# First FFN chunk's inputs and 28 weight tiles loaded in attention's last chunk, and the head of the FFN stage taken row tile by row tile

## The chip, the cores and the metric

One Trainium2 chip, one core. The metric is the device time of one execution in microseconds (us). Rows and times of the profile come from one profiled execution, and `L1301` means line 1301 of the kernel before. The engines are PE (TensorE; its weight loads are listed as PEld), DVE (VectorE), ACT (ScalarE), POOL (GpSimd) and SP (SyncE, which here only issues DMAs; its issues are listed as SPq). TensorE's granted clock is 1.00 at 2.4 GHz and 0.50 at 1.2 GHz.

## The reference

A transformer layer on x of 4096 rows by 512 columns, in float32:

```
q, k, v = split(x @ Wqkv);  q, k = layernorm(q) * q_scale, layernorm(k) * k_scale    # over all 512 columns
ctx = softmax(causal(q_h @ k_h.T / sqrt(32))) @ v_h      for each of 16 heads of 32 columns
x   = layernorm(x + ctx @ out_W)
h   = silu(x @ Wg.T) * (x @ Wu.T)       # Wg, Wu: 2048x512 integers minus 128, times a scale per row
x   = layernorm(x + h @ Wd.T)           # Wd: 512x2048, made in the same way
```

## The kernel before

The kernel is three stages, each a block of five instruction streams, with a barrier of all engines between them. `project` makes q, k and v and writes them to DRAM, each in a high and a low part, and turns the 48 integer weight tiles of the FFN (16 inner tiles by gate, up and down, 256 KB each) into floats in DRAM (`wq`). `attend` runs four groups of four heads; in each it takes the 8 query chunks of 512 rows in order, and for chunk n the key blocks of 128 rows up to the diagonal, so that the last chunk has 32 steps. A step is two score products, two exponentials on ACT, the weighting with the values on PE, and a sum on DVE (`total`). Key blocks of 512 rows lie in SBUF (`keys`, 64 KB per partition) with three query buffers (`queries`, 8 KB each); SP reloads each for the next group once its last scores are made. `store` sends a chunk's context and its sums to DRAM; the sums of chunk 0 are inverted inside `attend`, those of chunks 1 to 7 in `finish`.

`finish` is the FFN stage, in 8 chunks of 512 rows. A chunk has 16 inner tiles ("ic": gate and up into two `slot` banks at L1301, Silu on ACT at L1372, the product with up and the split on DVE at L1457 to L1465, and the down product into the four `y` banks at L1312). The first half of the layer for the next chunk is placed between the inner tiles ("o": output projection L1275, "t": transposes L1285). For chunk 0 nothing lies ahead to place it in, so it stands as a head in front. Its steps are these:

- SP loads the context (`cp_lo`, L1156), the inverses spread over partitions (`y_raw`, L1167), the residual rows (`x_res`, L1161), the scales, and then the weights, tile by tile (L1196, L1201).
- DVE scales the context (`context`: L1406, cast L1408, low part L1410) in two halves of 256 rows; each half raises `c_ready`.
- PE projects a half: 24 products of 128x512 into two banks (12 for each 128 rows).
- DVE adds the residual (L1437), takes the statistics (L1416 to L1421), POOL the root (L1243), DVE normalises (L1426).
- PE transposes a half, ACT writes the high part (L1353), DVE the low part (L1449), which frees the `slot` banks for the first gate product.

Ahead of its first inner tile PE loads a flag (`value_load`, L1339) and branches to one of two copies of the whole FFN program, with or without full float32 products; the flag is made at the start of `finish` from the weights' largest magnitude (L1391 to L1397). ACT waits for the inverses of chunks 1 to 7 (`inv_stored`) before its first Silu, since they pass through the tile `hidden`.

## Time and profile before

| | us |
|---|---|
| median of 3 runs | 2382.1 (2381.18 to 2382.73) |
| the profiled execution | 2378.85 |
| its span, first to last instruction | 2377.1 |
| last product of attention ends | 1531.06 |
| first projection product of the head | 1546.34 |
| first gate product | 1572.41 |
| first down product | 1581.79 |

PE is busy for 2304.8 us of the span (97%), DVE 75%, ACT 54%, POOL 10%. `project` takes some 330 us, `attend` some 1200, `finish` some 845. From 1581.79 on the chain that ends last is PE alone apart from short pieces: an inner tile of gate, up and down takes 5.44 us each time. All times in the text count from the start of the span.

### The profile page before, as it was taken

How to read it: one execution, taken by the hardware profiler on the slowest of the kernel's cores; microseconds unless marked ns; L12 is line 12 of the kernel's file. 1: busy time of each engine (PE TensorE's matmuls, PEld its weight loads, DVE VectorE, ACT ScalarE, POOL GpSimd, SP SyncE). 2: the span in 40 equal slices, each digit the busy share in tenths (PEclk: the TensorE clock that was granted, in tenths of full speed). 3: DMA queues.
4: the chain of work that ended last, by engine and by line, in shares of the span. 5: the costliest groups of instructions: out<-in, count | busy, mean ns of one | idle time of the engine just before them, and what ended most of it. 6: DMA issues, size and time to landing. Idle time of an engine off the chain costs nothing. (4 is left out here: it accounts for less than half of the span.)

```text
span 2377.1 us, 34417 instructions
## 1 busy us (share of the span) xinstructions
PE 2304.8 (97%) x12578; PEld 1421.6 (60%) x12578; DVE 1775.6 (75%) x1822; ACT 1291.7 (54%) x1631; POOL 246.1 (10%) x269
## 2 busy tenths in 40 slices
PE   8999979999999999999999999789999999999997
PEld 7888844444444444444444444268888888888885
DVE  7767748998889988899888998745646556565554
ACT  4444458888888888888888888611111111111111
POOL 2111111110111101211011110000000000000000
PEclk9999989999999999999999999989999999999998
DMA  7767794101811008110081100181111021110100
GB/s 253 255 238 251 236 259 97 44 6 24 169 46 44 8 22 171 42 45 11 19 174 42 42 14 6 52 285 36 36 36 54 19 72 36 37 53 18 36 18 18
DMA packets 126879, 197.52 MB, mean 83 GB/s; under 512 B 15064, under 2 KB 40152, under 8 KB 126688
## 3 DMA queue, kind: packets, MB, share of 16 engines
q1 hardware_dynamic: 126704, 195.25, 28.9%
q8 instruction: 102, 1.67, 0.3%
q14 instruction: 73, 0.60, 0.1%
HBM read 122.83 MB, written 72.37 MB: 82 GB/s over the span
## 5 line engine op out<-in xcount | busy, mean ns | idle before, releaser
L968 ACT ACTIVATE probs<-score 128x1024 f32<-128x1024 f32 (+3 forms) x1152 | 1000.1, 969 | 174.3 <-PE score L880 172.3
L1031 DVE TENSOR_TENSOR total<-total,probs 128x2048 f32<-128x2048 f32 (+3 forms) x468 | 983.6, 2102 | 79.5 <-POOL probs L842 22.1
L880 PE MATMUL score<-queries,keys 98*128 98x512 f32 (+3 forms) x2304 | 641.4, 406 | 11.6 <-issue 6.5
L880 PEld LDWEIGHTS score<-queries,keys 98*128 98x128 f32 x2304 | 380.3, 189 | 433.4 <-ACT probs L968 350.0
L1372 ACT ACTIVATE hidden<-slot,gate_scale_sb 128x512 f32<-128x512 f32 x128 | 88.3, 690 | 624.7 <-PE slot L1301 624.7
L896 PE MATMUL ctx_acc<-probs,values 128*32 128x512 f32 (+3 forms) x3584 | 421.5, 561 | 0.0
L1457 DVE SCALAR_TENSOR_TENSOR hidden<-slot,up_scale_sb,hidden 128x512 f32<-128x512 f32 x128 | 96.0, 750 | 258.4 <-ACT hidden L1372 258.4
L842 POOL TENSOR_SCALAR_AFFINE_SELECT probs<-probs 128x512 f32<-128x512 f32 x128 | 167.5, 1310 | 1005.7 <-ACT probs L968 1005.7
L1301 PE MATMUL slot<-xt_hi,wg_sb 128*128 128x512 f32 x512 | 201.6, 394 | 5.2 <-issue 5.2
L896 PEld LDWEIGHTS ctx_acc<-probs,values 128*32 128x32 f32 x3584 | 85.4, 108 | 193.9 <-issue 148.9
L1312 PE MATMUL y<-wd_sb,h_hi 128*128 128x512 f32 x512 | 199.4, 389 | 1.4 <-DVE h_lo L1465 1.4
L1301 PE MATMUL slot<-xt_lo,wg_sb 128*128 128x512 f32 x512 | 200.0, 391 | 0.0
L1312 PE MATMUL y<-wd_sb,h_lo 128*128 128x512 f32 x512 | 199.3, 389 | 0.0
L1301 PE MATMUL slot<-xt_hi,wu_sb 128*128 128x512 f32 x512 | 199.2, 389 | 0.0
L1301 PE MATMUL slot<-xt_lo,wu_sb 128*128 128x512 f32 x512 | 199.2, 389 | 0.0
L344 PE MATMUL acc<-w_hi,x_hi 128*128 128x512 f32 x384 | 163.4, 425 | 7.2 <-DVE w_lo L495 7.2
L344 PE MATMUL acc<-w_hi,x_lo 128*128 128x512 f32 x384 | 150.9, 393 | 0.0
L344 PE MATMUL acc<-w_lo,x_hi 128*128 128x512 f32 x384 | 150.4, 392 | 0.0
L896 PE MATMUL ctx_acc<-probs,first_values 128*32 128x512 f32 (+3 forms) x1024 | 132.2, 588 | 0.7 <-ACT ctx_out L957 0.7
L1243 POOL TENSOR_TENSOR rstd<-veps,minus_half 128x1 f32<-128x1 f32 x64 | 36.7, 573 | 803.2 <-DVE veps L1421 803.2
L1301 PEld LDWEIGHTS slot<-xt_hi,wg_sb 128*128 128x128 f32 x512 | 96.7, 189 | 25.6 <-issue 5.6
L1312 PEld LDWEIGHTS y<-wd_sb,h_hi 128*128 128x128 f32 x512 | 96.1, 188 | 22.1 <-DVE h_lo L1465 2.2
(103 smaller groups left out, 2066.8 us busy)
## 6 DMA issues: line engine op xcount, KB each, us to landing
keys<-k_hi SPq DMA_DIRECT2D x64, 256.0 KB
queries<-q_hi SPq DMA_DIRECT2D x64, 256.0 KB
wq_int<-in_wq SPq DMA_DIRECT2D x48, 256.0 KB, 3.2
wq_float<-wq_f SPq DMA_DIRECT2D x48, 256.0 KB, 2.8
x_raw<-in_x_t SPq DMA_DIRECT2D x32, 256.0 KB, 3.6
v_rows<-v_out SPq DMA_DIRECT2D x32, 256.0 KB, 2.2
q_hi<-part_hi SPq DMA_DIRECT2D x32, 256.0 KB, 2.5
q_lo<-part_lo SPq DMA_DIRECT2D x32, 256.0 KB, 2.8
```

The costliest lines, as they stand in the source:

```text
L344: ins = pe.matmul(bank[:], x[:, par, dc, rows], w[:, dc, m * D:(m + 1) * D], start=dc == 0 and a == 0, stop=dc == DC - 1 and a == 2)
L842: pool.affine_select(out=view, in_=view, compare_op=ALU.is_ge, fill=0.0, base=0, pattern=[[0, HG], [1, P]], channel_multiplier=-1).then_in ...
L880: ins = pe.matmul(score[u % RING][:, i, cut(t):], keys[0:ROWS, kb // ST, h, kb % ST * P:(kb % ST + 1) * P], queries[0:ROWS, q_buffer[ch], ...
L896: ins = pe.matmul(ctx[h * HD:(h + 1) * HD, n0:], value(kb)[:, h * HD:(h + 1) * HD], probs[:, t % PB, h, n0:], start=t in first, stop=t in ...
L968: act.activation(probs[:, t % PB, 2 * p:2 * p + 2, cut(t):], score[u % RING][:, :, cut(t):], ACT.Exp).then_inc(exped, 1)
L1031: dve.tensor_tensor(into, into, now, ALU.add).then_inc(added, 1)
L1243: pool.tensor_tensor(rstd[:, k, st:st + 1], veps[:, k, st:st + 1], minus_half[:], ALU.pow).then_inc(rooted[k], 1)
L1301: ins = pe.matmul(slot[pos % 2][q][:], v(w[:, i, dc * P:(dc + 1) * P]), v(x[:, par, dc, :]), start=dc == 0 and a == 0, stop=dc == DC - 1 a ...
L1312: ins = pe.matmul(y[st][:], v(x[:, i % 2, st * P:(st + 1) * P]), v(wd[:, i, :]), start=i == 0 and a == 0, stop=i == IC - 1 and a == 1)
L1372: act.activation(hidden[:, i % 2, :], slot[pos % 2][0][:], ACT.Silu, scale=gate_scale[:, i:i + 1]).then_inc(gated, 1)
L1457: dve.scalar_tensor_tensor(hid, slot[pos % 2][1][:], up_scale[:, i:i + 1], hid, ALU.mult, ALU.mult)\
```

## The change

- The context, residual rows and inverses of chunk 0, and the first 7 blocks of four weight tiles each (28 of 48 tiles), are issued by SP inside `attend`'s last group. They go to the places of what has just been used for the last time: query buffers 0 and 1, and `keys`, one 8 KB block for each weight block. The other 5 weight blocks are loaded in `finish`, as 1 MB DMAs.
- The scales are loaded after group 0 of attention.
- The store of attention's last chunk moves behind the barrier, to the start of `finish`.
- Both flags are made at the end of `project`: one more reduction on DVE, a second transpose, and a reduction of twice the length.
- In the head PE loads its flag and branches at once, ahead of the head. The head goes by row tiles of 128 into the `y` banks, each with a semaphore of its own, and not by halves.
- The sums of chunks 1 to 7 pass through the second `x1` buffer, so that ACT has no wait on their inverses; DVE inverts them after the head, and waits for the store in the residual of chunk 1.

```
+def ctx_load(sp, dr, keep, n, h):
+    sp.dma_start(keep["cp_lo"][:, h, :, :].bitcast(F32),
+                 dr["ctx"].rearrange("(g r) s -> r g s", r=P)[:, :, bass.ds(n * CH + h * HC, HC)]).then_inc(keep["ctx_in"][h], 16)
...
+def inv_load(sp, dr, keep, n):
+    for h in range(HG):
+        sp.dma_start(keep["y_raw"][h * HD:(h + 1) * HD, :, :],
+                     dr["inverse"].rearrange("n (g h) s -> n h g s", h=HG)[bass.ds(n, 1), h, :, :]
+                     .to_broadcast([HD, NG, CH])).then_inc(keep["inv_ready"], 16)
...
+def weight_load(sp, dr, keep, to, j):
+    sp.dma_start(to.bitcast(F32), dr["wq"].rearrange("(b t) p d -> b p t d", t=ST)[j]).then_inc(keep["w_in"][j], 16)
...
+            dve.wait_ge(whole_done, 2 + WT * NCH)
+            dve.tensor_reduce(check[:, 1:2], whole[:], AX.X, ALU.max).then_inc(fin, 1)
...
+            dve.tensor_reduce(check_top[:], turn[0][0:1, 0:2 * P].rearrange("a (k p) -> a k p", k=2), AX.X, ALU.max).then_inc(fin, 1)
...
+                if g == NG - 1:
+                    sp.wait_ge(scored, 2 * NS * g + 2 * (last[NCH - 2] + 1) + Q_CREDIT)
+                    sp.nop(nofuse=True)
+                    for h in range(HALF):
+                        ctx_load(sp, dr, keep, 0, h)
+                    for h in range(HALF):
+                        x_load(sp, io, keep, 0, h)
+                store_chunk(sp, dr, keep, g, NCH - 2)
...
+            sp.dma_start(keep["gate_scale"][:], io["gate_scale"]).then_inc(keep["small_in"], 16)
+            sp.dma_start(keep["up_scale"][:], io["up_scale"]).then_inc(keep["small_in"], 16)
+            sp.dma_start(keep["whole"][:], io["down_scale"].rearrange("(a h) -> a h", a=1).to_broadcast([P, D]))\
+              .then_inc(keep["small_in"], 16)
...
-            store(sp, NG - 1, NCH - 1)
             sp.wait_ge(inverse_stored, 16 * NG + 16)
+            sp.nop(nofuse=True)
+            sp.wait_ge(scored, 2 * NS * (NG - 1) + 2 * (key_end[NCH - 1] + 1) + Q_CREDIT)
+            sp.nop(nofuse=True)
+            inv_load(sp, dr, keep, 0)
+            for b in range(2):
+                sp.wait_ge(keep["wq_stored"][b], 16 * (3 * IC // 2) + 16)
+            for j in range(FRONT):
+                sp.wait_ge(scored, 2 * NS * (NG - 1) + 2 * (key_end[j] + 1) + Q_CREDIT)
+                sp.nop(nofuse=True)
+                weight_load(sp, dr, keep, keep["w_front"][:, j * ST:(j + 1) * ST, :], j)
...
-            ctx_load(sp, 0, 0)
-            inv_load(sp, 0)
-            ctx_load(sp, 0, 1)
-            x_load(sp, 0, 0)
-            x_load(sp, 0, 1)
+            store_chunk(sp, dr, keep, NG - 1, NCH - 1)
             for b in range(2):
                 sp.wait_ge(keep["ctx_stored"][b], 32 * (NCH // 2) * NG + 32)
             sp.dma_start(sums_flat[:, REST].rearrange("p (n s) -> p n s", s=FLAT), flat_rest("sums")).then_inc(sums_in, 16)
-            sp.dma_start(gate_scale[:], io["gate_scale"]).then_inc(small_in, 16)
-            sp.dma_start(up_scale[:], io["up_scale"]).then_inc(small_in, 16)
-            sp.wait_ge(checked, 1)
-            sp.dma_start(down_scale[:], io["down_scale"].rearrange("(a h) -> a h", a=1).to_broadcast([P, D])).then_inc(small_in, 16)
-            for b in range(2):
-                sp.wait_ge(keep["wq_stored"][b], 16 * (3 * IC // 2) + 16)
-            for i in range(2):
-                for k, to in enumerate((wg, wu, wd)):
-                    sp.dma_start(to[:, i, :].bitcast(F32), dr["wq"][3 * i + k]).then_inc(w_in[i], 16)
+            for j in range(FRONT, BLOCKS):
+                weight_load(sp, dr, keep, w_back[:, (j - FRONT) * ST:(j - FRONT + 1) * ST, :], j)
...
-            pe.wait_ge(ident_ready, 1)
-            pe.wait_ge(checked, 1)
-            pe.transpose(y[0][0:1, 0:P], check[:], ident[:]).then_inc(check_turned, 1)
+            wide = pe.value_load(keep["flags"][0:1, 1:2], min_val=0, max_val=1)
...
+            def head():
+                def out(st):
+                    pe.wait_ge(c_ready, st // HALF + 1)
+                    out_rows(y[st], st // HALF, st % HALF).then_inc(head_out, 1)
+                def turn(st):
+                    pe.wait_ge(normed[0], st + 1)
+                    for dc in range(DC):
+                        ins = pe.transpose(slot[st // HALF][st % HALF][:, dc * P:(dc + 1) * P],
+                                           x1[0][:, st, dc * P:(dc + 1) * P], ident[:])
+                    ins.then_inc(slot_full if st % HALF else head_turned, 1)
+                out(0)
+                out(1)
+                pe.wait_ge(ident_ready, 1)
+                for st in range(ST):
+                    if st + 2 < ST:
+                        out(st + 2)
+                    turn(st)
...
-            for pos, (kind, i) in enumerate(head):
-                if kind == "o":
-                    project_out(pos, pos, 0, i)
-                else:
-                    transpose(pos, pos, 0, 0, i)
-            pe.wait_ge(checked, 4)
-            wide = pe.value_load(keep["flags"][0:1, 1:2], min_val=0, max_val=1)
...
-            act.wait_ge(inv_stored, 16)
+            for st in range(ST):
+                act.wait_ge(slot_full if st % HALF else head_turned, st // HALF + 1)
+                act.activation(tile_of(xt_hi, 0, st), chunks_of(slot[st // HALF][st % HALF]), ACT.Copy).then_inc(high_ready, 1)
...
+            def low_rows(st):
+                dve.wait_ge(high_ready, st + 1)
+                ins = dve.tensor_tensor(tile_of(xt_lo, 0, st), chunks_of(slot[st // HALF][st % HALF]),
+                                        tile_of(xt_hi, 0, st).bitcast(F32), ALU.subtract)
+                if st % HALF:
+                    ins.then_inc(slot_free, 1)
+            for h in range(HALF):
+                context(dve, keep, 0, h)
+            for st in range(ST):
+                dve.wait_ge(head_out, st + 1)
+                dve.wait_ge(x_res_in[st // HALF], 16)
+                dve.tensor_tensor(x1[0][:, st, :], y[st][:], x_in[:, st // HALF, st % HALF, :], ALU.add).then_inc(summed[0], 1)
+                norm_begin(0, 0, 0, st, LN_EPS)
+                if st > 1:
+                    low_rows(st - 2)
+                norm_end(0, 0, 0, st)
+                if st % HALF:
+                    dve.sem_inc(half_used, 1)
+            low_rows(ST - 2)
+            low_rows(ST - 1)
...
+            keep["w_front"] = at("w_front", [P, FRONT * ST, D], keys_at, F32R)
+            keep["y_raw"] = at("y_raw", [P, ST, D], keys_at + 56 * KIB)
+            keep["cp_lo"] = at("cp_lo", [P, HALF, NG, HC], queries_at, F32R)
+            keep["x_res"] = at("x_res", [P, HALF, HALF, D], queries_at + 8 * KIB)
```

TensorE, the start of `finish`. `ow_hi`, `ow_lo` are the output projection's weights, `y` and `slot` PSUM banks. Before, where the head meets the first gate product:

```order
L1285 MATMUL slot<-ident,x 128x128 [waits normed0,slot_free]
L1285 MATMUL slot<-ident,x 128x128 x7
L1339 TENSOR_LOAD flags [waits checked]
L1339 ISA x2
L1341 COMPARE_AND_BRANCH
L1301 MATMUL slot<-xt_hi,wg_sb 128x512 [waits w_in0,slot_free]
```

and of the changed kernel, from the barrier on:

```order
L1286 UNCONDITIONAL_BRANCH [waits barrier_Pool_Activation_PE_DVE_SP_release]
L1289 TENSOR_LOAD flags
L1289 ISA x2
L1385 COMPARE_AND_BRANCH
L1296 MATMUL y<-ow_hi,cp_hi 128x512 [waits c_ready]
...
L1317 MATMUL slot<-ident,x 128x128 [waits normed0]
L1317 MATMUL slot<-ident,x 128x128 x3
L1352 MATMUL slot<-xt_hi,w_front 128x512 [waits w_in0,slot_free]
```

The flag's load and the branch stood between the last transposes and the first gate product; they now stand between the barrier and the first projection product.

ScalarE, the first Silu of `finish`. Before:

```order
L1353 ACTIVATE xt_hi<-slot 128x4x128 [waits slot_full]
L1353 ACTIVATE xt_hi<-slot 128x4x128
L1372 ACT_TABLE_LOAD [waits h_ready,slot_full]
L1372 ACTIVATE hidden<-slot,gate_scale_sb 128x512 [waits inv_stored]
```

and of the changed kernel:

```order
L1421 ACTIVATE xt_hi<-slot 128x4x128 [waits head_turned]
L1421 ACTIVATE xt_hi<-slot 128x4x128 [waits slot_full]
L1416 ACT_TABLE_LOAD [waits h_ready]
L1416 ACTIVATE hidden<-slot,gate_scale_sb 128x512 [waits slot_full]
```

The load of Silu's table had the wait for the first gate product (`slot_full`) in front of it; now that wait is behind it, and `h_ready` starts at 2, so the load waits for nothing.

SyncE, the end of `attend` in the changed kernel:

```order
L854 DMA flat<-sums 128x16 [waits ctx_stored0]
L111 DMA cp_lo<-ctx 128x4x256 [waits scored]
L111 DMA cp_lo<-ctx 128x4x256
L117 DMA x_res<-in_x 128x2x512 x2
L138 DMA sums<-sums_out 4x512 [waits sums_taken]
L142 DMA ctx<-ctx_out 128x512 [waits ctx_taken]
L866 DMA inverse<-flat_inv 128x16 [waits inverted]
L124 DMA y_raw<-inverse 32x4x512 [waits inverse_stored,scored]
L124 DMA y_raw<-inverse 32x4x512 x3
L131 DMA w_front<-wq_float 128x4x512 [waits scored,wq_stored0,wq_stored1]
L131 DMA w_front<-wq_float 128x4x512 [waits scored] x6
```

Before, this place had only the stores, the load of `flat` and the store of `inverse`; the loads came after the barrier.

## Rows read from the trace of the kernel before

**Rows 1.** Chain of waits, 1500 to 1600 us (start us, us, what)

```profile
1535.40 7.48 DMA y_raw<-inverse
...
1568.34 9.43 issue
...
1583.90 3.63 PE slot L1301 x16
```

**Rows 2.** Timeline, the hand-over (start, us, engine, line, operation, [idle before <-releaser])

```profile
1531.12 0.69 DVE L1018 COPY sums_out<-sums_acc 128x512 f32<-128x512 f32 x1 [1.19 <-PE sums_acc L915]
...
1532.48 0.39 SPq L713 DMA_DIRECT2D ctx<-ctx_out  x1
...
1533.43 0.06 DVE L1385 MEMSET minus_half<- 128x1 f32 x1 [1.61 <-PEq L643]
...
1538.27 4.42 SPq L1188 DMA_DIRECT2D gate_scale_sb<-in_gate_scale  x1
...
1542.98 1.23 DVE L1406 TENSOR_TENSOR y_raw<-cp_lo,y_raw 128x1024 f32<-128x1024 f32 x1 [7.31 <-DMA y_raw<-inverse]
...
1546.34 0.77 PE L1275 MATMUL slot<-ow_hi,cp_hi 128*128 128x512 f32 x1 [11.33 <-DVE cp_lo L1410]
...
1549.24 2.95 DVE L1497 RECIPROCAL hidden<-hidden 128x448 f32<-128x448 f32 x1
...
1551.17 0.54 PE L1275 MATMUL slot<-ow_hi,cp_lo 128*128 128x512 f32 x1
```

**Rows 3.** Timeline, the project stage's end and attention's first product

```profile
325.09 0.68 DVE L533 TENSOR_REDUCE norm_max<-norms_k 128x1 f32<-128x512 f32 x1
...
327.21 0.14 DVE L576 CAST flags<-flag_f 1x1 int32<-1x1 f32 x1
```

**Rows 4.** Timeline of TensorE, same place

```profile
333.21 5.89 PE L880 MATMUL score<-queries,keys 98*128 98x512 f32 x16 [6.52 <-issue]
```

**Rows 5.** Timeline, the head's second half

```profile
1559.91 1.29 DVE L1437 TENSOR_TENSOR x<-slot,x_res 128x512 f32<-128x512 f32 x2 [0.21 <-PE slot L1275]
...
1561.44 0.69 DVE L1416 BATCH_NORM_STATS2 stats<-x 128x6 f32<-128x512 f32 x1 [0.24 <-DVE x L1437]
...
1562.53 0.68 DVE L1416 BATCH_NORM_STATS2 stats<-x 128x6 f32<-128x512 f32 x1
...
1564.59 0.55 DVE L1426 TENSOR_SCALAR x<-x,mv,rstd 128x512 f32<-128x512 f32 x1 [0.44 <-POOL rstd L1243]
1565.05 1.28 DVE L1449 TENSOR_TENSOR xt_lo<-slot,xt_hi 128x512 fp32r<-128x512 f32 x2
```

**Rows 6.** Timeline of TensorE, the head's end to the first down product

```profile
1559.85 1.06 PE L1285 MATMUL slot<-ident,x 128*128 128x128 f32 x8
1565.28 1.94 PE L1285 MATMUL slot<-ident,x 128*128 128x128 f32 x8 [4.37 <-DVE x L1426]
1572.41 0.77 PE L1301 MATMUL slot<-xt_hi,wg_sb 128*128 128x512 f32 x1 [5.19 <-issue]
...
1580.94 0.39 PE L1301 MATMUL slot<-xt_lo,wu_sb 128*128 128x512 f32 x1
1581.79 0.50 PE L1312 MATMUL y<-wd_sb,h_hi 128*128 128x512 f32 x1 [0.46 <-DVE h_lo L1465]
```

**Rows 7.** Timeline of ScalarE, same place

```profile
1567.26 1.09 ACT L1353 ACTIVATE xt_hi<-slot 128x512 fp32r<-128x512 f32 x2 [5.17 <-PE slot L1285]
1577.78 1.28 ACT L1372 ACT_TABLE_LOAD   x1 [9.43 <-issue]
```

**Rows 8.** Stretches: engines' busy time, then granted clock, DMA share, GB/s

```profile
1533.00:1535.00 2.00, 0.36 (x1) 0.08 (x1) 0.75 (x2) 0.00 (x0) 0.50 (x2) 0.85 0.45 157
...
1564.00:1566.00 2.00, 0.72 (x4) 0.75 (x5) 1.56 (x4) 0.00 (x0) 0.56 (x1) 0.78 1.05 402
...
1574.00:1576.00 2.00, 2.00 (x8) 1.58 (x7) 0.00 (x0) 0.00 (x0) 0.00 (x0) 0.66 1.07 387
```

**Rows 9.** TensorE in two last chunks of attention, groups 0 and 3 (same columns)

```profile
588.00:632.00 44.00, 44.00 (x264) 1.00 0.94 181
...
1482.00:1526.00 44.00, 44.00 (x266) 1.00 0.01 1
```

250 lines of the change are left out of this document (117 added, 133 removed).

## The prediction

> **What bounds the kernel now.** I read the chain of waits first, then the timelines round the place it names. TensorE is busy for 97% of the span, and from the first down product at 1581.79 us on the chain is TensorE alone. The change leaves that part as it is, so it can only move the moment at which it begins. What lies ahead is a hole: attention's last product ends at 1531.06, the first projection product starts at 1546.34 and the first gate product at 1572.41 [rows 2, 6]. The chain of waits names the hole's parts: 7.48 us for the inverses' load, later 9.43 us as "issue" in front of the first Silu [rows 1]. That second piece is not one wait: TensorE stands still for 5.19 us, makes the first gate at half clock, and then ScalarE loads a table for 1.28 us [rows 6, 7].
>
> So I rebuild the path from the end of attention to the first down product. All times are on the clock of before; what the project stage adds is put on at the end.
>
> **1. From attention to the first projection product.** Before, VectorE's last copy ends at 1531.81, SP issues two stores until 1532.87, the barrier opens and VectorE works at 1533.43, that is 0.56 later. Then the loads land and the context is scaled at 1542.98 [rows 2]. Now the stores are behind the barrier, so it opens by VectorE's copy, and the loads have landed: context, rows and inverses are issued between some 1465 and 1485. VectorE can scale from 1531.81 + 0.56 + some 0.4 for the memset ahead of it, so from about 1532.75. From the start of the scaling to the first product it took 1546.34 - 1542.98 = 3.36 [rows 2], so the data would allow 1536.1.
>
> But TensorE now has the flag's load and the branch here. Two places show what that costs. At the start of attention, where the same two instructions stand behind the barrier, it is 333.21 - 327.35 = 5.86 us from the end of VectorE's last copy to the first product [rows 3, 4]. In front of the first gate product it is 5.19 us, with data there for about the last 3 of them [rows 6, 7]. I take the first, as it has the barrier in it: 1531.81 + 5.86 = **1537.67**. The wait for the load's landing has become a wait for the branch, and 1.6 us of the gain are lost in it. Against this stands a page: the Trainium skill's "Advanced Engine Details and Errata" (Control Flow Timing) gives about 108 ns for a compare-and-branch. By it the data would come last, and the start would be 1536.1. "Runtime: NRT & Kernel Launch" (Instruction fetch mechanics) says that a taken branch to a far target stalls on its fetch, and with that the trace agrees by its 5.19 and 5.86 us.
>
> **2. The head.** A row tile needs 12 products. Before, the first 12 ran at half clock, and the twelfth ended at 1551.17 + 0.54 = 1551.71, so 5.37 after the first began [rows 2]. TensorE has by then stood still for 6.6 us, and the clock had fallen in the stretch 1533 to 1535, some 3.4 us behind its last product [rows 8]; so half clock again: first tile ready at 1543.04, add at 1543.1. From here VectorE and GpSimd's root are the chain, since TensorE gives a tile each 2.7 us at full clock (12 x 0.227, as 16 products take 3.63 [rows 1]). One tile on VectorE is: add 0.69, gap 0.24, from statistics to the start of the normalisation 1564.59 - 1562.53 = 2.06, normalisation 0.55 with the next starting 0.46 after its start [rows 5]. That is 3.45 for each of three tiles and 3.54 for the last: 1543.1 + 10.35 + 3.54 = 1557.0. The low part of earlier tiles (0.69 each) lies in the 0.8 us in which VectorE waits for the root, and costs nothing; without that cover two of them would add 1.4.
>
> Then the last four transposes (0.14 later, 0.97 at half clock, half of 1.94), high part 0.63, low part 0.72 and 0.05 of waits [rows 5 to 7]: first gate product at **1559.5**, against 1572.41. Nothing else is late there: weights, flag and scales have been there for long. The clock: after the third tile's transposes TensorE has only 4 short products in each of two bursts, with gaps of about 1.3, 3 and 1.5 us. Before, after the transposes that end at 1560.91, it fell some 4.2 us later in 1564 to 1566 (0.78 in the row), and the gate product began at half clock, until about 1575.4 [rows 6, 8]. I take half clock again.
>
> **3. First gate to first down.** Before, from 1572.41 to the end of the second gate-and-up at 1580.94 + 0.23 it took 8.76 us; the down product began only at 1581.79, as the high and low parts were late by the table load [rows 6, 7]. Now the table load waits for nothing and lies beside the first gate product: 0.62 gained, and not 1.28, since TensorE's second tile comes last then. DVE's reciprocal for chunks 1 to 7 (2.95 us [rows 2]) moves behind the head, to 1559.4 to 1562.4, while the first Silu ends at about 1565.3: covered, by 2.9 us. First down product: 1559.5 + 8.76 = **1568.26** against 1581.79, a gain of 13.5.
>
> **4. The project stage.** The second flag's reduction of 128x512 stands in VectorE's row of reductions ahead of the flag, where nothing covers it: 0.6 to 0.68 [rows 3]. The second transpose and the reduction of twice the length are small, estimated 0.1 and 0.13. Cost 0.9, bounds 0.6 and 1.5.
>
> **5. In attention.** SP issues some 10 MB more beside chunk 7 of group 3. The same chunk of group 0 has that traffic already, for the next group: DMA share 0.94 against 0.01, 264 products in 44 us against 266 [rows 9]. The two differ by 0.8% at most and by where the stretch is cut; I take 0, bounds 0 and 0.5 us. A gain is excluded, as these engines wait for none of these loads. SP's queue: the scales' issues (4.42 us for one where the DMA queue was full [rows 2]) stand ahead of group 1's loads, which have most of chunk 7 to land in: 0. The last weight block is issued with the last scores, near 1526; even an issue of 4.4 us would end before 1531.81. The weights of `finish`, 5 MB, are first needed in inner tile 9, 50 us into the chunk: 0.
>
> **Sum.** 13.5 - 0.9 = 12.6 us. Span 2377.1 - 12.6 = 2364.5; the profiled execution, 2378.85, lies 3.3 below the median 2382.1, and I carry the difference over to the median: **2369.5 us**, 0.53% faster. The measurement can tell some 0.2%, 4.8 us.
>
> **Rivals.**
>
> *A: the clock holds through the head's end.* The short transposes keep it up. For: a gap of 1.3 and 3 us is shorter than the 4.2 after which it fell. Against: 1.1 us of work in 7. Then transposes take 0.43 less and the first gate pair 7.25 (32 x 0.227) and not 8.76: 2367.5.
>
> *C: the head is longer.* Branch, tile chain and clock each come out at their worst: the root is 0.55 to 0.78 us and might be longer, the first gate may run at half clock for 5 us as the first projection did and not 3 (1.0 more), the branch up to 3 us more. Gain 4 to 9: 2373 to 2378.
>
> *D: slower.* The loads into `keys` and the query buffers slow attention's last chunk, by contention for SBUF or memory. From 1472 to 1531 they would have to stretch 59 us by 21% to eat the gain, and by 29% to make it slower by over 0.2%: 2387 or more. It decides from 0.21 us per us; [rows 9] show under 0.01.
>
> *E: it does not do what it says.* The inverses of chunk 0 land late, as SP's queue holds them back behind weights or stores. Then the head starts near 1546 as before and only steps 2 and 3 gain (1.3 of tiling, 3.4 of branch, 0.6 of table, less 0.9): about 2378. Against: 45 us lie between the inverses' store and the barrier, and the load took 7.48 [rows 1].
>
> **Chances.** Forecast 0.47, A 0.22, B 0.12, C 0.10, D 0.04, E 0.05. The range takes the forecast with its bounds and A and B. Low: A and B together (2.0 + 1.6), and a first tile whose clock rises after 3 us (1.0 less): 2365.0. High: 0.6 more in the project stage, 1.0 of longer half clock, 0.9 in the tile chain, 0.5 in attention, and half of C's branch: 2374.5. Faster by over 0.2%: forecast, A, B and most of C, 0.88; within 0.2%: 0.08; slower: 0.04.
>
> **What would show it.** Barrier: VectorE scales the context within 1 us of its last copy. First projection product 5.9 us behind that copy, waiting for "issue" and not for VectorE. Adds on VectorE 3.4 to 3.5 us apart. First gate product some 21.8 us behind the first projection product (26.1 before), with a granted clock of 0.5; no 5 us of "issue" there, and the table load beside the gate product. Attention's chunk 7 as long as before. Flags written 0.9 us later. From the first down product on nothing differs. I am wrong if the first projection product starts by the data, if the clock stays up, or if attention's last chunk is longer by more than 1 us.

## The result, and the profile of the kernel after

| | before | after |
|---|---|---|
| median of 5 runs | 2382.1 us (2380.7 to 2384.46) | 2370.04 us (2369.36 to 2370.67) |
| profiled execution | 2378.85 us | 2370.67 us |
| its span | 2377.1 us | 2368.9 us |

After takes 0.9947 of before's time, with a 95% interval of 0.9936 to 0.9958. That is 12.1 us by the medians, against the 12.6 that the sum gave. The two profiled executions differ by 8.2 us only, and the sum had 12.6 for them too. The total came out right with terms that did not, so I go through them one after another.

The chain of waits of the kernel after, from attention's end to the first down product (start us, us, what):

```profile
1537.23 1.24 DVE y_raw L154
...
1539.22 1.24 DVE cp_lo L158
1540.46 1.48 issue
1541.94 5.02 PE y L1296 x12
1546.98 0.70 DVE x L1529
...
1550.07 0.69 DVE x L1529
...
1553.18 0.70 DVE x L1529
...
1556.20 0.69 DVE x L1529
...
1558.16 0.56 POOL rstd L1270
1558.75 0.56 DVE x L1447
...
1559.35 0.68 PE slot L1317 x4
1560.05 0.61 ACT xt_hi L1421
1560.68 0.70 DVE xt_lo L1519
1561.38 0.09 issue
1561.47 9.98 PE slot L1352 x32
```

No DMA is left in it. The 7.48 us for the inverses and the 9.43 us of "issue" of [rows 1] are gone, and 1.48 us of "issue" stand ahead of the first projection product: the data are ready at 1540.46 and TensorE comes later.

The timeline of the kernel after at the same place (start, us, engine, line, operation, [idle before <-releaser]); it answers to [rows 2, 6, 7]:

```profile
1535.72 0.69 DVE L1091 COPY sums_out<-sums_acc 128x512 f32<-128x512 f32 x1 [1.19 <-PE sums_acc L988]
...
1537.23 1.22 DVE L154 TENSOR_TENSOR y_raw<-cp_lo,y_raw 128x1024 f32<-128x1024 f32 x1 [0.39 <-issue]
...
1541.94 0.80 PE L1296 MATMUL y<-ow_hi,cp_hi 128*128 128x512 f32 x1 [6.29 <-issue]
...
1560.67 1.28 ACT L1416 ACT_TABLE_LOAD   x1
...
1561.29 2.94 DVE L1539 RECIPROCAL x_late<-x_late 128x448 f32<-128x448 f32 x1
...
1561.47 0.77 PE L1352 MATMUL slot<-xt_hi,w_front 128*128 128x512 f32 x1 [1.46 <-DVE xt_lo L1519]
...
1571.29 0.39 PE L1363 MATMUL y<-w_front,h_hi 128*128 128x512 f32 x1
```

VectorE scales the context 0.8 us behind the end of its last copy (1536.41); the first projection product follows 5.53 us behind that copy (14.53 before); the table load and the reciprocal lie beside the gate products; and the first down product has no idle time ahead of it.

Three stretches of the kernel after (engines' busy time, then granted clock, DMA share, GB/s):

```profile
1559.00:1561.00 2.00, 0.67 (x4) 0.42 (x4) 1.21 (x3) 0.93 (x2) 0.00 (x0) 0.71 0.02 7
1565.00:1567.00 2.00, 2.00 (x7) 1.56 (x6) 0.00 (x0) 0.00 (x0) 0.00 (x0) 0.58 0.83 159
1487.00:1531.00 44.00, 44.00 (x266) 18.30 (x269) 41.47 (x19) 37.58 (x41) 0.00 (x0) 1.00 0.53 168
```

The third answers to the second of [rows 9]: 266 products in 44 us with the DMA share at 0.53, as before with it at 0.01. The loads cost attention nothing: from the 1100th of its 1152 exponentials to VectorE's last copy it takes 61.7 us in all 14 traces, with the 8 MB of inverses and weights beside it (61.67 in after), without the 7 MB of weights (61.72 in e8, below) and without any of them (61.71 in before). The first two rows say that the clock fell as the last transposes ended, at about 1559.9, and rose in the middle of the gate pair, at about 1566.7.

The whole span by parts, each kernel from its own profiled execution:

| part | before | after | difference | predicted |
|---|---|---|---|---|
| start to the flags' copy done | 327.35 | 330.91 | +3.56 | +0.9 |
| to the end of VectorE's last copy | 1204.46 | 1205.50 | +1.04 | 0 |
| to the first projection product | 14.53 | 5.53 | -9.00 | -8.67 |
| to the first gate product | 26.07 | 19.53 | -6.54 | -4.24 |
| to the first down product | 9.38 | 9.82 | +0.44 | -0.62 |
| to the end of the span | 795.31 | 797.61 | +2.30 | 0 |
| sum | 2377.1 | 2368.9 | -8.2 | -12.6 |

Each row is the time from the event in the row above. Two of them were not in the forecast at all: the first, beyond 0.9, and the last. The last is the clearer one. In the FFN stage TensorE never waits, so 2.3 us more means slower products. The chain of waits shows which, in the kernel after:

```profile
1611.34 5.59 PE slot L1296 x24
```

and in the kernel before, the same 24 projection products inside a chunk:

```profile
1621.98 5.44 PE slot L1275 x24
```

There are 14 such blocks (two in each of the seven chunks that prepare the next one); 14 times 0.15 is 2.1 us.

### The profile page after: what moved, and what is told of

Read it like the earlier page. It is cut to its first block and busy times, and to the rows that moved or that the text cites. A ratio compares the mean times of both kernels' runs of the same rounds, so it can differ in the third digit from the quotient of the medians.

```text
span 2368.9 us, 34364 instructions
## 1 busy us (share of the span) xinstructions
PE 2308.9 (97%) x12556; PEld 1424.3 (60%) x12578; DVE 1775.2 (75%) x1821; ACT 1291.7 (55%) x1631; POOL 245.3 (10%) x269
## 5 line engine op out<-in xcount | busy, mean ns | idle before, releaser
L953 PE MATMUL score<-queries,keys 98*128 98x512 f32 (+3 forms) x2304 | 641.7, 406 | 12.1 <-ACTq L1025 6.2
L1352 PE MATMUL slot<-xt_hi,w_front 128*128 128x512 f32 x608 | 238.5, 392 | 1.5 <-DVE xt_lo L1519 1.5
L1352 PE MATMUL slot<-xt_lo,w_front 128*128 128x512 f32 x608 | 238.1, 392 | 0.0
L1352 PE MATMUL slot<-xt_hi,w_back 128*128 128x512 f32 x416 | 163.4, 393 | 0.0
L1352 PE MATMUL slot<-xt_lo,w_back 128*128 128x512 f32 x416 | 162.1, 390 | 0.0
L1352 PEld LDWEIGHTS slot<-xt_hi,w_front 128*128 128x128 f32 x608 | 115.1, 189 | 26.2 <-DVE xt_lo L1519 1.7
L1352 PEld LDWEIGHTS slot<-xt_lo,w_front 128*128 128x128 f32 x608 | 115.0, 189 | 23.9
L1363 PE MATMUL y<-w_front,h_hi 128*128 128x512 f32 x288 | 112.1, 389 | 0.0
L1363 PE MATMUL y<-w_front,h_lo 128*128 128x512 f32 x288 | 112.1, 389 | 0.0
```

The source lines that it names most:

```text
L953: ins = pe.matmul(score[u % RING][:, i, cut(t):], keys[0:ROWS, kb // ST, h, kb % ST * P:(kb % ST + 1) * P], queries[0:ROWS, q_buffer[ch], ...
L1352: ins = pe.matmul(slot[pos % 2][q][:], v(w[:, dc * P:(dc + 1) * P]), v(x[:, par, dc, :]), start=dc == 0 and a == 0, stop=dc == DC - 1 and ...
L1363: ins = pe.matmul(y[st][:], v(x[:, st * P:(st + 1) * P]), v(tile(i, 2)), start=i == 0 and a == 0, stop=i == IC - 1 and a == 1)
```

## The experiments

### Where the gain comes from: the loads, the branch, the weights

**e5_loads_in_ffn** is after with chunk 0's context, inverses and residual rows issued in `finish`, as before; weights, head and all else stay as in after. (This edit and those below are shortened: waits and loop bodies that go along with the lines shown are left out.)

```diff
 # attention's queue of SP
-ctx_load(sp, dr, keep, 0, h)      # for both halves
-x_load(sp, io, keep, 0, h)        # for both halves
-inv_load(sp, dr, keep, 0)
 # finish, SP
 store_chunk(sp, dr, keep, NG - 1, NCH - 1)
+ctx_load(sp, dr, keep, 0, 0)
+inv_load(sp, dr, keep, 0)
+ctx_load(sp, dr, keep, 0, 1)
+x_load(sp, io, keep, 0, 0)
+x_load(sp, io, keep, 0, 1)
```

> The changed kernel with the loads of the first chunk's context, inverses and residual rows back behind the barrier (after the last chunk's two stores); the weights stay early. Theory (these loads are the main gain): the inverses land 13 to 16 us behind VectorE's last copy of attention, the first projection product starts some 9 us later than in the changed kernel (14.5 behind the copy, not 5.53), the branch is hidden, and the whole is 8 to 10 us slower than the changed kernel, 2 to 4 faster than the kernel before. Rival (the weights' early load and the branch's place are the gain): 0 to 3 us slower than the changed kernel.

Measured: 2381.07 us (2378.12 to 2383.2, 10 runs), ratio to before 0.9996 (0.9986 to 1.0005), so 11 us slower than after, where 8 to 10 were expected. Its chain of waits has the DMA back:

```profile
1541.42 1.49 SPq L124
1542.91 0.04 issue
1542.96 8.04 DMA y_raw<-inverse
```

The first product starts 15.91 us behind the last copy, and copy to first down product is 45.10 us (34.88 in after). The issue of the four inverse loads (1.49 us) and the wait for their landing (8.04 us) are the path. So 10.2 of the 15.1 us that this stretch gained are these loads, and with them undone nothing measurable is left of the change. This stretch is still 4.9 us shorter than before, by the head in row tiles, the early flag and the table; in the profiled execution a later end of the project stage (4.7 us), a longer attention (1.9 us) and the slower products (2.3 us) more than take that back. What the first two of these are made of is told further down.

**e8_weights_in_ffn** is after with all seven `w_front` loads issued in `finish` ahead of the `w_back` loads.

```diff
 # attention's queue of SP
-for j in range(FRONT):
-    sp.wait_ge(scored, ...)
-    weight_load(sp, dr, keep, keep["w_front"][:, j * ST:(j + 1) * ST, :], j)
 # finish, SP
+for j in range(FRONT):
+    weight_load(sp, dr, keep, w_front[:, j * ST:(j + 1) * ST, :], j)
```

> The changed kernel with all 48 weight tiles loaded behind the barrier again; context, inverses and rows stay early. Theory: the weights' early load is worth nothing by itself, since the first block (1 MB) lands some 8 to 10 us behind the barrier and the first gate needs it 25 us behind it, and the others follow at 2.7 us each against 7.3 us of use: same time within 0.5 us, no wait on a weight block. Rival: gate products wait for blocks, or the inverses of chunks 1 to 7 land too late behind 12 MB of weights and chunk 1's projection waits: slower by 1 us or more.

Measured: 2371.14 us (2370.8 to 2372.33, 3 runs), ratio 0.9952 (0.9937 to 0.9968), not to be told from after. Copy to first down product is 34.72 us (34.88). The 28 weight tiles moved by the change gain nothing by their place: from the first gate product to the first down product it is 9.74 us (9.82), and from there to the end 797.7 (797.6), so no product waits for a block.

**e1_no_branch** is after without the flag's load and the branch on TensorE, **e7_before_no_branch** is before without them. The products are those of the copy that runs.

```diff
-wide = pe.value_load(keep["flags"][0:1, 1:2], min_val=0, max_val=1)
...
-with pe.If(wide):
-    program(lambda ap: ap.bitcast(F32))
-with pe.Else():
-    program(lambda ap: ap)
+program(lambda ap: ap)
```

> The changed kernel without the flag's load, the branch and the second copy of the FFN program on TensorE (the copy with full float32 products, which these inputs never take, is left out). In the changed kernel the first projection product starts 5.53 us behind VectorE's last copy, while the scaled context is there at 4.05. Theory (the branch comes last): the first product now waits for VectorE's low part and starts at 4.1 to 4.2 us behind the copy, the first down product comes 1.3 to 1.4 us sooner behind that copy (33.5 instead of 34.88), the whole 1.4 us faster. Rival (the branch is hidden, something else holds TensorE, such as the barrier): the start stays at 5.5, no change.

> The kernel before without the flag's load and branch in front of its first gate product (the full float32 copy of the FFN program is left out). Theory: the 5.19 us of idle there shrink to the 2.0 us until VectorE's low part is done, so 3.2 us faster; the gate products may keep half clock. Rival: the gate waits for weights or something else, and stays at 5.2.

Measured for e1: 2369.08 us (4 runs), ratio 0.9945 (0.9929 to 0.9962); by the whole time it can't be told from after, but the trace can: the first product starts 4.09 us behind the last copy, released by VectorE, and the first down product 32.90 us behind it (34.88). Of these 2.0 us the start gave 1.4. The rest is the clock, which moved against the work: the head takes 20.04 us (19.53), as half clock lasts until 1546.4 and the dense products began sooner, and the gate pair 8.78 (9.82), as half clock ended 3.1 us into it and not 5.2. Timeline of TensorE in e1:

```profile
1540.37 0.79 PE L1295 MATMUL y<-ow_hi,cp_hi 128*128 128x512 f32 x1 [4.84 <-DVE cp_lo L158]
```

Measured for e7: 2378.06 us (8 runs), ratio 0.9988 (0.9978 to 0.9999), a hair faster than before; 3.2 us were expected. Timeline of TensorE in e7:

```profile
1570.44 0.77 PE L1301 MATMUL slot<-xt_hi,wg_sb 128*128 128x512 f32 x1 [2.21 <-DVE xt_lo L1445]
```

The 5.19 us of "issue" of [rows 6] are 2.21 here, ended by the data. So the branch cost before 3.0 us in front of the first gate product, and costs after 1.4 in front of the first projection product, as the prediction read both places. But in e7 the gate pair up to the down product takes 10.69 us (9.38), since half clock lasts until about 1576.3, 5.9 us into the pair and not 3.0, so only 1.4 of the 3.0 us reach the first down product. Both experiments take out load, branch and the unused copy together; which of the three costs the time is not shown.

### The head

**e2_table_back** holds ScalarE's table load behind a wait that has long been satisfied when it comes.

```diff
 # ScalarE, ahead of the first Silu
+act.wait_ge(small_in, 48)
 over_chunks(act, body)
```

> The changed kernel with one idle wait more on ScalarE, by which Silu's table is loaded behind the first gate product again, as in the kernel before. Theory: the first high and low part of hidden come 1.28 us later than in the changed kernel; of that 0.47 us are free there (low part ready at 1570.51, TensorE free at 1571.29 less the overlap), so a gap of 0.5 to 0.8 us opens in front of the first down product. Rival: the table load was free before too, no gap.

Measured: 2372.06 us (2370.55 to 2374.35, 3 runs), ratio 0.9959 (0.9943 to 0.9975). Timeline of ScalarE and TensorE in e2:

```profile
1568.72 1.28 ACT L1416 ACT_TABLE_LOAD   x1 [7.29 <-PE slot L1352]
...
1572.73 0.50 PE L1363 MATMUL y<-w_front,h_hi 128*128 128x512 f32 x1 [0.43 <-DVE h_lo L1487]
```

The table load falls behind the wait for the first gate result, and the down product waits: 10.47 us from gate to down instead of 9.82, that is 0.65 more. The added wait had been met long before, so it cost no time itself; it only moved the load behind the wait for the first gate result. In after the load runs straight behind `xt_hi`.

**e3_by_halves** is after with the head in halves of 256 rows, as before, all else as in after.

```diff
 # TensorE
-for st in range(ST):
-    if st + 2 < ST:
-        out(st + 2)
-    turn(st)
+out(2)
+out(3)
+for p in range(HALF):
+    pe.wait_ge(normed[0], HALF * p + HALF)
+    for q in range(HALF):
+        turn(HALF * p + q)
```

(VectorE's side takes the adds, statistics and normalisations two at a time in the same way.)

> The changed kernel with its head by halves of 256 rows on VectorE and for the transposes, as before, and not by row tiles. Theory: from the first projection product to VectorE's last low part the changed kernel takes 19.4 us, the kernel before 22.8; by halves it is 22 to 23.5, so 3 to 4 us longer, all ahead of the first gate product. Rival: the tiling gains nothing, as the chain is bound by the same sum of VectorE's work: within 0.5 us of 19.4.

Measured: 2371.38 us (2368.66 to 2373.08, 3 runs), ratio 0.9954 (0.9938 to 0.997). First projection to first gate product is 21.60 us, 2.1 more than in after, where 3 to 4 were expected. But the gate pair takes 8.68 instead of 9.82. Half clock came and went sooner there: it began 4.0 us ahead of the first gate product (1560.53) and not 1.6, as TensorE stands still for 4.1 us ahead of its last eight transposes, and so it ended 2.8 us into the pair and not 5.2:

```profile
1562.00:1564.00 2.00, 2.00 (x8) 1.57 (x7) 1.28 (x1) 0.00 (x0) 0.00 (x0) 0.67 0.00 0
```

Copy to first down product is 35.67 us against 34.88: the tiling is worth 0.8 us net, and the runs' times can't show it.

**e6_busy_head** fills TensorE's gaps with products whose result is overwritten.

```diff
 # TensorE, behind the transposes of row tile st
+for _ in range({2: 10, 3: 6}.get(st, 0)):
+    pe.matmul(y[0][:], ow_hi[:, 0, 0:P], ow_lo[:, 0, :], start=True, stop=True)
```

> The changed kernel with 10 spare products of the output weights into a free PSUM bank behind the third row tile's transposes and 6 behind the fourth's, to keep TensorE at work until the first gate product. Theory: in the changed kernel the clock was down from about 1560.2 to 1566.6, and the first two gate-and-up pairs took 9.8 us; with TensorE busy the clock stays at 1.0 and they take 7.25, so 2.5 us faster. Rival: the clock falls for another reason, or the spare products delay the transposes by as much: no gain, or slower.

Measured: 2368.2 us (2366.76 to 2371.3, 4 runs), ratio 0.9945 (0.9929 to 0.9962). The stretch of the kernel after at 1559 to 1561 had clock 0.71; in e6 it is:

```profile
1559.00:1561.00 2.00, 1.94 (x12) 1.44 (x10) 1.22 (x3) 0.96 (x2) 0.00 (x0) 1.00 0.00 0
1561.00:1563.00 2.00, 1.93 (x9) 1.33 (x8) 2.00 (x2) 0.92 (x1) 0.00 (x0) 1.00 0.04 8
```

The clock holds, the gate pair takes 7.36 us (9.82), and copy to first down product is 31.99, 2.9 less than after. The spare products account for 2.5 of that. The other 0.4 lies ahead of them, in the first row tile, where half clock in this execution ended 3.4 us behind the first projection product and not 4.3. The whole time is 1.8 us less by the medians, and with five and four runs that is no more than suggested.

### The slower projection products

**e4_before_cp_low** was the first test: before with `cp_lo` and `cp_hi` allocated between `wu` and `wd`, near the places that they have in after.

```diff
 wu = sb("wu_sb", [P, IC, D], F32R)
+cp_lo = sb("cp_lo", [P, 2, NG, HC], F32R)
+cp_hi = sb("cp_hi", [P, 2, NG, HC], F32R)
 wd = sb("wd_sb", [P, IC, D], F32R)
```

> The kernel before with the two context tiles of the FFN stage moved in SBUF from 186 and 194 KB to 98 and 106 KB in a partition, nothing else. In the changed kernel 24 projection products inside a chunk take 5.59 us and not 5.44, 14 times, 2.1 us in all. Theory (placement of these tiles decides it): 5.59 us here too and the FFN stage 2.1 us longer than before. Rival (something else of the changed kernel): 5.44 as before, same time.

Measured: 2382.49 us (2380.83 to 2386.35, 8 runs), ratio 1.0004 (0.9993 to 1.0014), and blocks of 5.44 us. My theory was wrong: moving the context by some 88 KB did nothing. But the new places were not those of after: after has two more tiles of 64 bytes per partition (the scales) ahead of `keys`, and so everything behind lies 128 bytes higher. Meanwhile 5.59 was seen in e1, e2, e3, e5, e6 and e8 alike, so that branch, loads, table and tiling are not the cause. Two experiments moved nothing but these 128 bytes.

**e9_scales_behind**, after with the scales elsewhere:

```diff
 # ahead of keys
-"gate_scale": sb("gate_scale_sb", [P, IC], F32), "up_scale": sb("up_scale_sb", [P, IC], F32),
 # behind the buffers of the context's outputs
+keep["gate_scale"] = last.enter_context(nc.sbuf_tensor("gate_scale_sb", [P, IC], F32))
+keep["up_scale"] = last.enter_context(nc.sbuf_tensor("up_scale_sb", [P, IC], F32))
```

> The kernel after with one thing changed: the two tiles of scales (64 bytes per partition each) are allocated behind the context's buffers instead of ahead of keys, so that keys, w_front, cp_lo, cp_hi, x_res and y_raw lie 128 bytes lower, where keys lay before. Every operation stays. Open is why each block of 24 projection products inside a chunk takes 5.59 us in the kernel after (5.44 before, 14 blocks, 2.1 us in all). Theory: the place of cp_hi and cp_lo decides it, and the earlier experiment that moved them to 98.16 and 106.16 KiB in the kernel before (5.44) had them 128 bytes off the places of after; then the blocks take 5.44 us here and the kernel ends about 2 us earlier (ratio to before 0.9938). Rival: it has nothing to do with the 128 bytes; 5.59 stays and the time is that of after within 0.5 us.

**e10_before_pad**, the mirror:

```diff
 "whole": sb("whole", [P, D], F32),
+"pad": sb("pad", [P, 32], F32),
```

> The mirror: the kernel before with an unused tile of 128 bytes per partition ahead of keys, so that everything behind it (cp_hi, cp_lo, the weights, the transposed tiles) lies 128 bytes higher. Theory of the 128 bytes: blocks of 24 projection products take 5.59 us instead of 5.44, and the kernel takes about 2 us longer. Rival: 5.44 stays.

e10: the blocks take 5.59 us, and the FFN stage from the first down product 797.84 (795.31). The pad alone makes the blocks slow. (Its time, 2386.72 us, is that of a single run, 5 us above before's median; by the trace 2.5 of them are this, and the rest lies in attention, told further down.)

e9: the blocks take 5.44, as the theory said, and the kernel takes 2380.9 us (10 runs), ratio 0.9993 (0.9984 to 1.0003): 11 us slower than after, where I expected it 2 us faster. Its chain of waits:

```profile
1700.17 3.72 PE slot L1352 x16
...
1709.45 1.86 PE y L1363 x8
1711.31 5.44 PE slot L1296 x24
```

A gate-and-up pair of 16 products takes 3.72 us here and 3.63 in after, 8 down products 1.86 and not 1.81. The FFN stage takes 808.29 us instead of 797.61. What decides is not one operand's place but how the two operands of a product lie to each other. A product has a stationary operand, 128x128, which is loaded into the array as weights, and a moving one, 128x512, which streams through it. With ow and cp, and with a weight tile and h, the one named first is moving; with a weight tile and xt it is the other way round. In bytes modulo 256, with what the products took (mean distance of starts, from the timelines between 1660 and 1900 us; places worked out from the order of the allocations):

| product | kernel | modulo 256 | distance |
|---|---|---|---|
| ow, cp | before, e4 | 160, 160 | 0.2267, 0.2271 us |
| ow, cp | after | 160, 32 | 0.2332 |
| ow, cp | e10 | 160, 32 | 0.2333 |
| ow, cp | e9 | 160, 160 | 0.2267 |
| ow, cp | e11, below | 32, 32 | 0.2267 |
| w_front, xt | after | 32, 32 | 0.2268 |
| w_front, xt | e9 | 160, 32 | 0.2327 |
| w_back, h | after | 32, 32 | 0.2269 |
| w_back, h | e9 | 32, 160 (every second h_lo 32) | 0.2326 |
| w_front, h | e9 | 160, 160 (every second h_lo 32) | 0.2307 |
| w_back, xt | e9 | 32, 32 | 0.2279 |

Where all products around have operands that lie alike they start 0.2267 us apart, where they are 128 bytes off modulo 256 some 0.233, 2.8% more, whichever of the two is the moving one. The stage has 3,456 such products. In after 336 of them inside the chunks lie apart, in e9 nearly half. Neighbours of such products are a little slow too: the first four gate products behind each block in after, and the last two rows of the table, where fewer lie apart than the distance tells. So 0.0065 us for each product that lies apart is a lower bound: 10.6 us for e9, by the 1,632 of them from the first down product on, where the stage is 13.1 us longer than in the kernel e11 below. How the neighbours come to be slow was not tried.

**e11_scales_ahead** makes all alike: the scales stand ahead of `ow_hi`, so that `ow` lies at 32 too and all else stays.

```diff
 keep = {
+    "gate_scale": sb("gate_scale_sb", [P, IC], F32), "up_scale": sb("up_scale_sb", [P, IC], F32),
     "flags": sb("flags", [P, 2], I32), "ow_hi": ...
-    "gate_scale": sb("gate_scale_sb", [P, IC], F32), "up_scale": sb("up_scale_sb", [P, IC], F32),
```

> The kernel after with the two tiles of scales allocated ahead of flags and ow_hi, so that ow_hi and ow_lo lie 128 bytes higher (byte 16,672 instead of 16,544) and all else lies where it did. In bytes modulo 256 the weights ow_hi and ow_lo then lie at 32, as cp_hi, cp_lo, xt_hi, xt_lo, w_front and w_back do; in the kernel after ow lay at 160 and cp at 32. Theory, from five kernels: a product whose two operands lie at the same place modulo 256 starts 0.2267 us behind the one before, one whose operands differ by 128 starts 0.233 us behind. Then blocks of 24 take 5.44 us and every other product stays: 2.1 us off the FFN stage (first down product to the end 795.5 instead of 797.6). Rival: only cp_hi and cp_lo at 160 give the fast blocks (as in before and in the kernel with the scales behind); 5.59 stays, and the time is that of after.

Measured: 2366.12 us (2365.96 to 2370.55, 5 runs), ratio 0.9939 (0.9925 to 0.9952), by the medians 3.9 us less than after, of which the places explain 2.4. The rival, that only cp at 160 is fast, falls: cp lies at 32 here. Chain of waits:

```profile
1603.69 3.63 PE slot L1352 x16
1607.32 1.81 PE y L1363 x8
1609.13 5.44 PE slot L1296 x24
```

The FFN stage takes 795.22 us from the first down product on, 2.4 less than after and as before (795.31). It beats before clearly; that it beats after is shown by the trace's FFN stage, while by the whole time the intervals of the two ratios overlap.

**e12_all_three** is e11 with e6's spare products, and with eight more ahead of the flag's load, which alone are shown.

```diff
 pe.sem_inc(slot_free, FREE)
+for _ in range(8):
+    pe.matmul(y[0][:], ow_hi[:, 0, 0:P], ow_lo[:, 0, :], start=True, stop=True)
 wide = pe.value_load(keep["flags"][0:1, 1:2], min_val=0, max_val=1)
```

> The kernel e11_scales_ahead with the 10 and 6 spare products of e6_busy_head in the head, and with 8 spare products more (ow_hi by ow_lo into y[0], overwritten later) at the start of TensorE's FFN stage, ahead of the load of the flag. Expected: from the head as e6_busy_head had it, clock 1.0 at the transposes and the gate pair, first down product 2.5 to 3 us earlier against e11_scales_ahead. From the 8 products: they run in the wait for the branch, from about 0.2 us behind VectorE's last copy and at half clock for 3.4 us, so the clock rises earlier behind the first projection product, worth up to 2 us, if the load of the flag does not wait for them. Rival: the load and the branch begin only when the 8 products are done; then the first projection product comes about 3 us later than 5.5 us behind the last copy, and the kernel is no faster than e11_scales_ahead with e6's gain less 1 to 3 us.

Measured: 2366.62 us (2364.15 to 2369.47, 5 runs), ratio 0.9931 (0.9918 to 0.9945). Timeline of TensorE in e12:

```profile
1540.24 2.08 PE L1290 MATMUL y<-ow_lo,ow_hi 128*128 128x512 f32 x8 [1.25 <-PEq L708]
1545.15 0.80 PE L1298 MATMUL y<-ow_hi,cp_hi 128*128 128x512 f32 x1 [2.82 <-issue]
```

Neither theory holds. The eight products ran at full clock (0.26 us each), not at half, and the load did not wait for them: the first projection product still comes 5.40 us behind the last copy. Yet they gained nothing: TensorE stood still for another 2.82 us behind them, the clock fell in that gap, at about 1544.4, and the first projection products ran at half clock until about 1551. The head's spare products worked again (gate to down 7.37 us), and copy to first down product is 32.81 against 35.81 in e11.

## Why the prediction was right, point by point

**The hand-over** was right in kind and by 0.3 us in size: 5.53 instead of 5.86. The branch comes last; e1 shows that by the data it would have been 4.09, where I had 4.3 (1536.1). The same read at the start of attention is 5.38 in after. Rival B is out. The Trainium skill's "Advanced Engine Details and Errata" (Control Flow Timing) gives about 108 ns for a compare-and-branch. That does not cover this pair of a load and a branch past a long program: without it the first gate product came 3.0 us earlier (e7) and the first projection product 1.4.

**The head** was mis-sized: 19.53 us from the first projection to the first gate product and not 21.8. Four terms, each a little too long: the first tile 5.04 (5.43 to the add), since the clock rose after 4.3 us; three tiles at 3.09, 3.11 and 3.02 (3.45 each); the last tile's statistics and normalisation 3.10 (3.54); transposes, high and low part 2.17 (2.5). The 3.45 was made of pieces of the head by halves, where two tiles share VectorE and the root takes 0.79 us. In e3, which goes by halves again, the second root of a pair is 0.79 and the first 0.55; in after all four are 0.55, and the statistics start 0.72 behind the add's start and not 0.93. A step of a chain that is cut anew should be re-added from its shortest rows, with the longest as the bound.

**The clock at the head's end** was half right. The last four transposes ran at full clock, 0.67 us for four, where I had half. It fell as they ended, and the gate pair was cold: 9.82 us, more than the 8.76 that I had taken over from before, because the cold part lay wholly in it. Rival A is out; e6 shows what it would have been worth: 2.5 us in the pair, where I had 1.5 (and 0.4 in the transposes, which came without it).

**The table load** is hidden, and e2 puts 0.65 us on it (0.62 predicted). **The reciprocal** is covered: it ends at 1564.23, ahead of the first high part.

**The flags** cost 0.84 us, 0.9 predicted: from the last norm reduction's start to the flags' copy done it takes 2.26 us before (325.09 to 327.35) and 3.10 after (327.81 to 330.91). **But the project stage** ended another 2.7 us later in the profiled execution, ahead of anything the change touches. The last 48 of the stage's 1,152 products with the weights `w_hi` and `w_lo` and what follows them hold most of it: the 1,104th starts at 297.84 in before and 298.41 in after, and from there to the flags it takes 29.5 to 30.1 us in the four traces with the old flags and 30.8 to 33.6 in the ten with the new. The DMA share is 1.0 and more there, in both kernels from 295 to 321, and ScalarE waits there for stores of `part_lo` (2.6 us at once in after, 3.2 in before). Part of it may be the clock. In the kernel before, then in the kernel after (TensorE's busy time, clock, DMA share, GB/s):

```profile
318.00:320.00 2.00, 2.00 (x11) 1.00 1.05 403
```

```profile
318.00:320.00 2.00, 2.00 (x8) 0.50 1.01 382
```

TensorE has gaps of some 1.7 us there in both kernels, and in 5 of the 10 traces with the new flags (after, e1, e5, e8, e12) the clock was at half for some time in 317 to 321; in none of the four with the old ones. By 8 products against 11 in 2 us that costs up to some 1.5 us, an estimate. But e6 was late with no such fall at all, e2 with one near 306 only, and e3 (near 305) and e7 of the old kind (310 to 313) were not late with theirs, so the clock does not sort them. In e3, e9 and e11 the flags are done at 328.4 to 328.8, that is 0.3 to 1.5 us behind the four of the other kind (327.35 to 328.03), and in the other seven at 330.2 to 332.1. Less the 0.84 of the new flags, these three are like the four. Whether the change makes the late kind likelier, or ten and four executions only happened to fall so, is open. Nothing was run to settle it.

**Attention** cost 1.04 us, where I had bounds of 0 and 0.5. Not by the loads: the last chunk is as long as before. The first product comes 5.38 us behind the flags and not 5.86, and from it to the last copy attention is 1.5 us longer. All of that lies in its first 64 exponentials (66.2 us against 64.5); from the 64th on it takes 1133.9 to 1134.3 us in all 14 traces. There are two places. One is the half clock at the start: it lasted until about 348 and not 343, so that attention ran 11.8 us at it instead of 10.0. In e4, with the flags of before, it was 11.4 and in e11, with the new ones, 8.8, so it goes with the execution and not with the change. The other is a wait of TensorE at 384 for a small load, 0.88 us in after and none in before, in e12 the longest but one:

```profile
385.86 1.77 PE L953 MATMUL score<-queries,keys 98*128 98x512 f32 x6 [1.86 <-DMA queries<-shift]
```

Behind it e12 runs at 0.50 for some 7 us, and so does e10, behind a wait of 1.22 us; both kernels' attention is 3 to 4 us longer (1202.7 and 1203.5 us from its first product, against 1198.6 in before and 1200.1 in after). The wait alone does not tell whether the clock falls. It fell at 1.22 (e10), 1.86 (e12) and 2.05 (e5) and held at 0.88 (after) and 1.05 (e11), but in e6 it held at 1.69 (the wait, then the stretch behind it with the clock at 1.00):

```profile
385.87 1.64 PE L953 MATMUL score<-queries,keys 98*128 98x512 f32 x6 [1.69 <-DMA queries<-shift]
387.00:389.00 2.00, 1.71 (x13) 0.54 (x11) 0.74 (x1) 2.00 (x3) 0.21 (x1) 1.00 0.05 19
```

So the difference in attention between the profiled executions, up to 4.9 us, comes from its first 70 us, but for 0.4 us. Whether the change makes this wait likelier is open: of the four traces of the kind before only e10 has it, of the ten of the kind after all but e1 and e9.

**The FFN stage** was put at nothing, and costs 2.3 us. The step that failed is the sentence that from the first down product on nothing differs, by which the stage stood in the sum at nothing. The instructions are the same; their operands' places are not. I had not looked at where the tiles lie.

**The sum**: the stretch from the last copy to the first down product gained 15.1 us instead of 13.5, and FFN and attention gave 3.3 back. That the prediction came within 0.6 us of the median is luck. The span was forecast at 2364.5 us and measured at 2368.9, 4.4 more: the project stage ended 2.7 us later than forecast, attention took 1.0 and the FFN stage 2.3 more, against the 1.6 that the stretch between gained beyond the sum. And 3.9 us came back because the 3.3 us by which before's profiled execution lay under its median were carried over, while after's lay 0.6 above. In e11, whose FFN stage is as before's, the medians differ by 15.6 us. The range's upper end was also added up wrongly: its terms (0.6, 1.0, 0.9, 0.5 and 1.5) give 2374.0 us and not 2374.5, and neither end had a term for the places.

## What to carry to other kernels

Where a stage's start waits for a load of some 8 us, moving that load ahead of the barrier gains only until the next thing is late, so price what comes next (here the flag's load and the branch, 5.5 us behind the last copy). When allocations change, compare the places of the two operands of each product modulo 256 bytes before calling a stage untouched; here places 128 bytes off cost 2.4 us in after and 13.1 in e9. Fill short gaps of TensorE ahead of a dense stretch, but mind that they touch it: in e12 spare products that end 2.8 us before it gave nothing. Before reading a difference of 1 to 4 us off whole times, look in which part of the trace it arises; here most of the scatter sits in the end of one stage and the first 70 us of the next. And a change that moves work by 1 or 2 us moves it against the half-clock stretches too, which in e1, e3, e6 and e7 gave or took 0.4 to 1.6 us.

## What the runs showed of the hardware

- Rows of fp32r products of 128x512 whose moving and stationary operands lie alike modulo 256 bytes start 0.2267 us apart, rows in which they differ by 128 bytes 0.233 (before, after, e4, e9, e10, e11). Which offset it is, 32 or 160, makes no difference. Products that lie alike but stand among others that don't are slowed too (0.2307 and 0.2279 in e9). Why it is so, and what other differences do, was not tried.
- With the load of a flag and the branch past the copy that isn't taken, the first product starts 5.4 to 5.6 us behind VectorE's last copy in the FFN stage of after, e2, e3, e6, e8, e9, e11 and e12, against 4.09 without them (e1). At the start of attention, where no run took them out, it is 5.3 to 6.0 us behind the flags in all 14 traces. Eight products queued ahead of the load run in that time without making it later (e12: 5.40).
- In the head of after the clock fell at about 1559.9 (0.71 in the row of 1559 to 1561), 2.9 us behind two bursts of four transposes that ended at 1557.0, and just as four more ended; in before it fell 4.2 us behind the end of eight transposes [rows 6, 8]. In e12 eight dense products ahead of the flag's load put the fall off until about 1544 (0.84 in 1543 to 1545), and the first projection product at 1545.15 met half clock all the same. From half clock it took 4.3 us of dense products to rise in the head of after, 5.2 at the gate pair, and 11.8 at the start of attention. For the same place it differs between executions: in the head 3.4 (e6) to 6.0 (e1, e12), at attention's start 8.8 (e11) to 12.1 (e6).
- 168 GB/s of loads, 7.4 MB in 44 us at a DMA share of 0.53, beside dense attention cost no measurable time (266 products in 44 us with and without; the last 61.7 us of attention alike within 0.1 us in 14 traces).
